# Second layer of a two-layer decoder: the softmax's inverse sums spread by DMA in place of TensorE transposes, and the outputs scaled by GpSimd

## The reference

```python
# A1: 4 groups of keys and values, 16 query heads of 64, no mask
raw  = einsum('bsgwe,btge->bstgw', Q, K * 64**-0.5)
A    = einsum('bstgw,btge->bsgwe', softmax(raw, axis=2), V).reshape(n, s, 1024)
x    = layernorm(x + (X + A @ Wpost))
# X1: 8 heads of 64, 1024 keys from the context
sim  = einsum('bihd,bjhd->bhij', q, k) * 64**-0.5
out  = einsum('bhij,bjhd->bihd', softmax(sim), v).reshape(b, n, 512)
x    = layernorm(x + out @ Wout + bout)
```

## Time and profile before

| | |
|---|---|
| runs | 1192.88, 1193.17, 1196.08 us (median 1193.17) |
| profiled execution | 1193.53 us, of which span 1191.8 us |
| mean granted TensorE clock | 0.973 |
| busy: TensorE, weight loads | 1089.6 us (91%), 689.9 us (58%) |
| busy: VectorE, ScalarE, GpSimd | 744.2 us (62%), 550.5 us (46%), 111.3 us (9%) |
| chain that ended last | PE 74%, DVE 13%, issue 5%, ACT 4%, DMA 1% |

### The profile page before, as it was taken

How to read it: one execution, slowest core, us unless ns; L and a number is a source line. 1 busy time by engine, 2 the same in 40 slices (tenths; PEclk the granted TensorE clock), 3 DMA queues, 4 the chain that set the end, 5 groups by cost and what they waited for, 6 DMA issues and landing times.

```text
span 1191.8 us, 19630 instructions
## 1 busy us (share of the span) xinstructions
PE 1089.6 (91%) x7306; PEld 689.9 (58%) x7306; DVE 744.2 (62%) x1092; ACT 550.5 (46%) x1044; POOL 111.3 (9%) x133
## 2 busy tenths in 40 slices
PE   5999989888788988789889999999999999999997
PEld 3443443432222322368666777877778787788664
DVE  3432555589999998553336566466666776776257
ACT  2434335155455556722126566356644554466320
POOL 2001123020200000010000000010002000120020
PEclk9999889799899999899999999999999999999999
DMA  5614003210000000000035333114432633220001
GB/s 153 170 71 150 10 22 112 91 65 14 14 14 14 15 1 1 1 19 1 1 72 147 72 72 72 37 45 99 107 72 54 153 88 76 68 72 1 1 1 36
DMA packets 56493, 67.89 MB, mean 57 GB/s; under 512 B 14665, under 2 KB 35922, under 8 KB 56402
## 3 DMA queue, kind: packets, MB, share of 16 engines
q1 hardware_dynamic: 55234, 65.06, 20.9%
q10 hardware_dynamic: 1168, 1.57, 0.4%
HBM read 30.96 MB, written 13.63 MB: 37 GB/s over the span
## 4 chain that ended last, share of the span: by engine, by line
PE 74%; DVE 13%; issue 5%; ACT 4%; DMA 1%; SPq 1%; ACTq 0%; POOL 0%; DVEq 0%; POOLq 0%
PE p_ring L1725 11%; PE p_unit L1725 11%; PE p_out L1872 10%; PE p_ring L1769 9%; PE p_ring L1849 9%; PE p_ring L1746 6%; PE p_out L1838 5%; PE p_ring L1815 5%; DVE halves L1496 4%; DVE prob_a L1510 2%; PE p_ring L1793 2%; DVE x L1695 2%; PE p_unit L1950 2%; ACT prob_b L1296 1%; PE p_unit L1904 1%
## 5 line engine op out<-in xcount | busy, mean ns | idle before, releaser
L1310 ACT ACTIVATE prob_a<-p_ring 128x1024 f32<-128x1024 f32 x128 | 130.5, 1022 | 97.4 <-PE p_ring L1815 97.1
L1475 DVE TENSOR_REDUCE nmax<-p_ring 128x2 f32<-128x1024 f32 (+1 forms) x128 | 156.0, 1219 | 30.1 <-PE p_ring L1769 30.1
L1496 DVE TENSOR_REDUCE halves<-p_ring 128x2 f32<-128x1024 f32 x128 | 155.8, 1220 | 27.5 <-PE p_ring L1793 27.1
L1296 ACT ACTIVATE prob_b<-p_ring,nmax 128x512 f32<-128x512 f32 (+1 forms) x192 | 158.6, 837 | 30.9 <-DVE nmax L1475 30.7
L1328 ACT ACTIVATE probT_b<-p_ring 128x512 f32<-128x512 f32 x144 | 84.5, 598 | 189.5 <-PE p_ring L1849 187.9
L1769 PE MATMUL p_ring<-stacks 128*128 128x512 f32 x512 | 150.8, 417 | 9.2 <-ACT prob_b L1296 5.4
L1529 DVE COPY probT_b<-p_ring 128x512 f32<-128x512 f32 x112 | 77.1, 688 | 114.6 <-PE p_ring L1849 114.3
L1849 PE MATMUL p_ring<-ident,prob_b 128*128 128x128 f32 x1024 | 134.6, 274 | 0.3 <-ACT probT_b L1328 0.3
L1849 PEld LDWEIGHTS p_ring<-ident,prob_b 128*128 128x128 f32 x1024 | 116.2, 141 | 23.6 <-issue 15.2
L1815 PE MATMUL p_ring<-x_q,x_kq 32*128 32x512 f32 x512 | 119.4, 648 | 2.3 <-DVE halves L1496 2.1
L1769 PEld LDWEIGHTS p_ring<-stacks 128*128 128x128 f32 x512 | 86.9, 189 | 26.2 <-ACT prob_b L1296 10.0
(11 more groups left out here) (208 smaller groups left out, 1537.9 us busy)
## 6 DMA issues: line engine op xcount, KB each, us to landing
stacks<-splitH_b SPq DMA_DIRECT2D x80, 128.0 KB, 2.3
stacks<-splitL_b SPq DMA_DIRECT2D x80, 128.0 KB, 2.4
stacks<-x_kd SPq DMA_DIRECT2D x32, 256.0 KB, 4.6
x_kd<-early SPq DMA_DIRECT2D x8, 512.0 KB, 3.8
x_v<-x_vd SPq DMA_DIRECT2D x8, 512.0 KB, 4.1
x_vd<-early SPq DMA_DIRECT2D x6, 512.0 KB, 2.8
a_st<-a_image SPq DMA_DIRECT2D x32, 64.0 KB, 2.7
x_kd<-xT SPq DMA_DIRECT2D x4, 512.0 KB, 3.1
```

What stands on the lines that cost most here:

```text
L1296: ins = nc.scalar.activation(prob_b[:, n % NP_SLOTS, a * 512:a * 512 + w_all], p_scores[:, n % 2, a * 512:a * 512 + w_all], ACT.Exp, bias= ...
L1310: nc.scalar.activation(prob_place(key), slot_of("S2", key), ACT.Exp, accum_out=x0_sums[:, m:m + 1]).then_inc(done["E2"], 1)
L1475: nc.vector.tensor_reduce(nmax[:, n % 4, 0:heads], src, AX.X, ALU.max, negate=True).then_inc(done["M"], 1)
L1496: nc.vector.tensor_reduce(to, src, AX.X, ALU.max, negate=True).then_inc(done["M1"], 1)
```

## The change

For 23 of the 24 groups the unit `rb`, `rwide` and ScalarE's copy go. VectorE's RC is the reciprocal alone. A new step RS on SyncE, in the same round, writes the inverse sums with two DMAs (one a head, 128 partitions x 4 elements of 4 bytes) to a small DRAM tensor `b_sums`, so that a head's 512 values lie in a row. Three rounds later the step RL loads each row back, repeated on 64 partitions, into one of two slots of `spread`. VectorE copies `p_out` unscaled into `outT_b` (OC) at the place where ON was, and the next group's AV waits for OC. ON is now done by GpSimd, in place on `outT_b`, and is scheduled one round after OC. The last group of all keeps `rb`; there VectorE does OC and then ON in place.

```diff
@@ stream @@
+        while spreads and spreads[0][0] <= n:
+            sched.add(*spreads.pop(0)[1])
+        while scaled and scaled[0][0] <= n:
+            sched.add(*scaled.pop(0)[1])
...
             if i == TT - 1:
-                late.append(("ON", L, b, g))
+                late.append(("OC", L, b, g))
+                scaled.append((n + 2 if (L, b, g) != last_group else n, ("ON", L, b, g)))
...
             sched.add("RC", *group)
-            sched.add("UP", "rb", *group)
-            pending.append(("rb", *group))
-            placed = True
+            if group == last_group:
+                sched.add("UP", "rb", *group)
+                pending.append(("rb", *group))
+                placed = True
+            else:
+                sched.add("RS", *group)
+                spreads.append((n + 3, ("RL", *group)))
@@ SyncE @@
+                if kind == "RS":
+                    G = group_no[key]
+                    slot, turn = G % 2, G // 2
+                    wait(sp, "RC", *key)
+                    if turn:
+                        sp.wait_ge(sums_spread[slot], 16 * 2 * turn)
+                    for a in range(2):
+                        sp.dma_start(b_sums[slot, a].rearrange("(i p) -> p i", p=128), rsum[:, slot, :, a],
+                                     allow_slow_non_contiguous=True).then_inc(sums_stored[slot], 16)
+                if kind == "RL":
+                    G = group_no[key]
+                    slot, turn = G % 2, G // 2
+                    sp.wait_ge(sums_stored[slot], 16 * 2 * (turn + 1))
+                    if turn:
+                        wait(sp, "ON", *groups[G - 2])
+                    for a in range(2):
+                        sp.dma_start(spread[64 * a:64 * a + 64, slot, :], b_sums[slot, a].partition_broadcast(64))\
+                          .then_inc(sums_spread[slot], 16)
@@ GpSimd @@
+                elif kind == "ON" and key != last_group:
+                    g = key[2]
+                    G = group_no[key]
+                    wait(pool, "OC", *key)
+                    pool.wait_ge(sums_spread[G % 2], 16 * 2 * (G // 2 + 1))
+                    nc.gpsimd.tensor_tensor(outT_b[:, g, :], outT_b[:, g, :], spread[:, G % 2, :], ALU.mult)\
+                      .then_inc(done["ON"], 1)
@@ VectorE @@
-                elif kind == "ON":
+                elif kind == "OC":
                     L, b, g = key
-                    G = group_no[key]
-                    wait(dve, "UA", "rb", *key)
                     wait(dve, "AV", *key, TT - 1, parts(key[0]) - 1)
...
-                    nc.vector.tensor_tensor(outT_b[:, g, :], p_out[:, :], spread[:, :], ALU.mult)\
+                    nc.vector.tensor_copy(outT_b[:, g, :], p_out[:, :]).then_inc(done["OC"], 1)
+                elif kind == "ON" and key == last_group:
...
+                    wait(dve, "UA", "rb", *key)
+                    wait(dve, "OC", *key)
+                    wait(dve, "ON", *groups[G - 1])
+                    nc.vector.tensor_tensor(outT_b[:, g, :], outT_b[:, g, :], spread[:, G % 2, :], ALU.mult)\
                       .then_inc(done["ON"], 1)
@@ TensorE @@
                     if i == 0 and part == 0 and G:
-                        wait(pe, "ON", *groups[G - 1])
+                        wait(pe, "OC", *groups[G - 1])
```

More of the change, by code:

```diff
@@ L266, in stream @@
     heads = [list(c) for c in chains]
-    late = []
+    late, scaled, spreads = [], [], []
+    last_group = tiles[-1][:3]
     def empty():
@@ L287, in stream @@
     n, crowded = 0, False
-    while n < len(tiles) + LAG + 1 or any(heads) or pending or late:
+    while n < len(tiles) + LAG + 1 or any(heads) or pending or late or scaled or spreads:
         if n < len(tiles):
@@ L578, in decoder @@
     bank_no = {u: i % 4 for i, u in enumerate(broad)}
-    groups = [key for kind, key in sched.steps if kind == "ON"]
+    groups = [key for kind, key in sched.steps if kind == "OC"]
+    last_group = groups[-1]
     early_places, early_uses = {}, [0] * EARLY
@@ L691, in decoder @@
         early = [early0[:, :, :], early1[:, :, :], xT[:, :, T:2 * T]]
+        b_sums = nc.dram_tensor("b_sums", (2, 2, T), F32).ap()
         x1_kd = nc.dram_tensor("x1_kd", (B, 4, 128, NKV), F32).ap()
@@ L759, in decoder @@
         x1_bo = put("x1_bo", [128, C])
-        spread = put("spread", [128, 512])
+        spread = put("spread", [128, 2, 512])
         m_b1 = put("m_b1", [128, NE + 1])
@@ L787, in decoder @@
             "E2": "turned_probs_ready", "TM": "later_keys_cleared", "PV": "values_added", "KF": "operands_rounded",
-            "RC": "sums_inverted", "ON": "outputs_scaled", "UP": "unit_ready",
[1 row of a table added]
             "UA": "unit_emptied_by_act", "UD": "unit_emptied_by_dve",
@@ L797, in decoder @@
         a0_stacked = [sem(f"a0_stacked{s}") for s in range(HELD)]
+        sums_stored = [sem(f"sums_stored{s}") for s in range(2)]
+        sums_spread = [sem(f"sums_spread{s}") for s in range(2)]
         a0_spread = [sem(f"a0_spread{b}") for b in range(B)]
@@ L1357, in _ @@
                         G = group_no[u[1:]]
-                        if G:
-                            wait(act, "ON", *groups[G - 1])
-                        ins = nc.scalar.activation(spread[:, :], p_unit[:, :], ACT.Copy)
+                        wait(act, "ON", *groups[G - 2])
+                        ins = nc.scalar.activation(spread[:, G % 2, :], p_unit[:, :], ACT.Copy)
                     elif u[0] == "xT" and u[1] == "X0":
@@ L1534, in _ @@
                     ng = LAYERS[key[0]]["G"]
[L1535 to L1542, removed]
-                elif kind == "ON":
+                    if G >= 2:
+                        dve.wait_ge(sums_stored[G % 2], 16 * 2 * (G // 2))
+                    ins = nc.vector.reciprocal(rsum[:, G % 2, :, 0:ng], sums[:, G % 2, :, 0:ng])
+                    if key == last_group:
+                        link(ins)
+                        ins = nc.vector.tensor_copy(rwide[:, :, :].rearrange("p i (a r) -> p i a r", a=ng),
+                                                    rsum[:, G % 2, :, 0:ng].unsqueeze(3).to_broadcast([128, TT, ng, 128 // ng]))
+                    ins.then_inc(done["RC"], 1)
+                elif kind == "OC":
                     L, b, g = key
-                    G = group_no[key]
-                    wait(dve, "UA", "rb", *key)
                     wait(dve, "AV", *key, TT - 1, parts(key[0]) - 1)
```

## The result

The changed kernel takes 1219.56 us (median of three runs, 1214.98 to 1224.92; a fourth, at 1233.30, counts as a slow run and is left out), the kernel before 1194.24 in the same measurement: ratio 1.0213, 95% interval 1.0184 to 1.0242. Forecast was 1184, with a range of 1178 to 1194. The profiled execution is the quickest of the runs, 1214.98 us, span 1213.2, which is 21.4 more than the span before; so the profile shows somewhat less than the median's loss of 25.

The account below looks back on a forecast made before the run. TensorE was taken to bound the kernel in the second layer's attentions. Gain 15.0 - 2.7 - 1.0 - 1.0 - 0.5 - 0.3 = 9.5 us, so 1193.5 - 9.5 = 1184.0 us, with an 8-in-10 range of 1178 to 1194.

Parts of the forecast that it names:

- Small writes: SyncE's writes of 1024 4 B elements per group: landing 4.9 us flat to 39 us linear, taken near flat.
- For traffic in the way of the stack loads: Small writes' effect on the stack loads: a charge of 1.0 us, bounds 0 and 4.
- Rival B: SyncE: stack loads queue behind the late spread load if a write takes over 22 us; 1214 us at 24; chance 0.05.
- Transposes, 15.0 us: TensorE, 23 groups losing their transposes: 15 save 0.74 us each, 8 save 0.49, together 15.0 us.
- Exchange of units, 2.7 us given back: TensorE's units sharing one PSUM bank: waits grow from 7.9 to 10.6 us in the new order.
- three second halves wait for the statistics: Output projection's second half waiting for VectorE's statistics: three places instead of one, 3 x 1.2 = 3.6 us.
- projections behind another: TensorE: three projections still stand one round behind another one, waiting 3.4 us.
- transposes of x: TensorE: 2.0 us for neighbouring transposes and the router's unit; 1.6 us for first transposes waiting for VectorE's normalisation.
- GpSimd: a multiply: GpSimd's scaling of the output, sized as half of its 128x1024 add: 1.25 us.
- Rival A: GpSimd multiplies stop VectorE's two-input operations: eight subtractions x 1.2 = 9.6 us, time 1193; chance 0.08.
- Output projections waiting for GpSimd, 1.0: TensorE at three output projections waiting for GpSimd's multiply: 0.7, 0 and 0.3 us, together 1.0.
- read-modify-write: DMA writes below 512 B: would only move the write's landing inside the three rounds before its load.

Follow-up runs that it names:

- Experiment 2: The kernel before plus each group's two scattered 4 B-element writes on SyncE, read by nobody, sums still spread by TensorE: 1223.39 us, ratio 1.0247.
- experiment 11: The changed kernel with the written elements 512 B apart and the spread load reading another tensor (outputs wrong, time only): 1181.08 us, ratio 0.9897.
- experiment 8: The kernel before plus the same touching, unread writes, issued on ScalarE's DMA queue one round later: 1234.84 us, ratio 1.0345.
- experiment 5: The changed kernel with inverse sums written as 16 B pieces and GpSimd's multiply reading them with a stride, results right: 1183.03 us, ratio 0.9915.
- Experiment 6: The changed kernel with 16 B pieces and strided multiply, and the place of rb left empty so the order of units is kept: 1181.85 us, ratio 0.9899.
- 1: The changed kernel with the small write as one DMA of 128 pieces of 32 B (sums in wrong order, time only): 1181.42 us, ratio 0.9886.
- Experiment 3: The kernel before with the raw copy on VectorE and the multiply on GpSimd, sums still spread by TensorE: 1192.61 us, ratio 0.9977.
- experiments 7 to 10: The kernel before plus unread 4 B-element writes: 512 B apart 1195.31 us; touching, on ScalarE's queue 1234.84; 64 B apart 1197.85; 16 B apart 1199.75.
- experiment 7: The kernel before plus the unread scattered writes on SyncE, each 4 B element 512 B from the next: 1195.31 us, ratio 1.0020.

## Why the prediction was wrong

**The step that failed** is "Small writes ... I take near the flat end ... For traffic in the way of the stack loads I charge 1.0 (bounds 0 and 4)". Its bracket for one write, 4.9 to 39 us, held: the two writes seen in the chain of waits took 9.64 and 11.88 us, and SyncE waited up to 11.3. Two things in it were wrong. First, the value at the flat end was an argument about latency, taken from 128 elements, for a write of 1024. A bracket that wide should have gone into the range. Second, the price on other transfers was bounded by 4 us with no row behind it. Experiment 2 puts the writes without any reader at 28 us, and experiment 11 puts them at 38 us in this kernel.

**Rival B** had the right place and the wrong condition. It let the loss begin at 22 us per write, from the slack of SyncE's queue in A1. In X1 three rounds are 8.5 us, so a write of 10 us was late there already. That its time of 1214 lies near the measured 1219.56 is luck. And it priced only the queue, while the transfers beside the writes suffered whoever issued them (experiment 8). It had a chance of 0.05, with 0.04 for its kind, on a price that no row excluded.

**The other terms held, in sum.** Without the 1.0 for small writes they give a gain of 10.5 us. The four versions with quick writes gained 10.8 (experiment 5), 11.9 (6), 13.1 (11) and 14.1 us (1). One slip: 1178, the low end of the range, is 1193.5 - 15.0 and so leaves out the exchanges too; with them in, as the text says, it is 1181. In detail:

- Transposes, 15.0 us: in X1 a pair of rounds fell from 6.39 to 5.65, as forecast. In A1 it fell by more, 6.62 to 5.70. TensorE, one such pair from one block of output matmuls to the next, before and then after:

```profile
729.85 1.97 PE L1872 MATMUL p_out<-probT_b,a_v 128*64 128x128 f32 x32
731.74 0.66 PE L1950 MATMUL p_unit<-ident,rwide 128*128 128x128 f32 x4
...
736.47 0.77 PE L1872 MATMUL p_out<-probT_b,a_v 128*64 128x128 f32 x10
```

```profile
724.19 1.97 PE L1915 MATMUL p_out<-probT_b,a_v 128*64 128x128 f32 x32
...
729.89 0.88 PE L1915 MATMUL p_out<-probT_b,a_v 128*64 128x128 f32 x12
```

- Exchange of units, 2.7 us given back: three second halves wait for the statistics for 3.7 us together (forecast 3.6), projections behind another 2.3 (forecast 3.4), transposes of x 1.4 and 0.5 (forecast 2.0 and 1.6). That is 7.9 us, no more than before, where 10.6 was forecast: nothing was given back. Experiment 6 fits: it can't tell the total from nothing.
- GpSimd: a multiply takes 1.28 us (forecast 1.25). Rival A had the mechanism right and the price wrong. Experiment 3 shows it, 2.18 us in place of 1.27 for a multiply and 2.05 in place of 1.22 for a subtraction, but in two places a subtraction and not in eight, and there was no loss. In the changed kernel the subtractions, themselves late, all took 1.21 to 1.23 us.
- Output projections waiting for GpSimd, 1.0: 6.4 in the changed kernel, and none in experiment 5. The first wait, 2.52 us, has stack issues of 3.93 us for two (at 741.87) ahead of the spread load, where 1.1 is usual; at the second, 3.92 us, the load came late behind its write. This term depended on the one that failed. The second in the chain of waits:

```profile
873.30 11.88 DMA b_sums<-rsum
```

- Not in the sum at all: the clock after a stall. TensorE's busy time fell by 3.8 us only, 1089.6 to 1085.8, where the four versions with quick writes have 1075.6 to 1078.7 with the same matmuls. So some 7 to 10 us of the loss are most likely matmuls at the lower clock.

The Trainium skill (DMA: Bandwidth & Descriptors, Specifications) says that below 512 B a transfer is done as read-modify-write. I had it move only the landing. The runs bear out that a small write can be dear, but not by its size alone: 4 B elements 512 B apart landed in 2.0 us, and 16 B pieces side by side did too. That neighbouring pieces wait for each other's read-modify-write would fit experiments 7 to 10; no run shows the inside of it.

## What to carry to other kernels

A DMA that scatters single 4 B elements so that neighbours touch in DRAM is not a 2 KB transfer: here it held up the others for up to about ten microseconds, whichever queue issued it. Let each partition write at least 16 B that lie together (the smallest piece that was tried and found quick), and let the reader undo the order with a strided view. When an operation is new to a kernel, price what it does to its neighbours as well as its own length, and if no row bounds it, let the range say so: measure it first by adding it alone to the kernel before, with nobody reading it.

## What the runs showed of the hardware

- 4 B elements side by side: 1223.39 us, 16 B apart 1199.75, 64 B apart 1197.85, 512 B apart 1195.31, against 1194 to 1196 without them; landing 3.5, 2.3 and 2.0 us for the last three.
- Such writes on one queue stretched another queue's packets from 20.9 to 25.5% of the engines' time. Behind them the DMA engines, 0.87 busy, moved 23 GB/s (187 with the elements 512 B apart), and at another place loads whose packets were all on record by 794.6 us had not landed before 802.4.
- Half as many such elements cost more (1238.17), not less.
- After waits of TensorE of 6.25 to 8.08 us the next four score matmuls took 2.04 to 2.06 us in place of 1.17 (four places in three runs); in experiment 2 the granted clock was 0.50 from 816 to 820 us, after a wait of 7.93 us. After a wait of 3.11 us (experiment 7, granted clock 1.00) they took 1.16.
- A GpSimd multiply that started 0.17 us after a VectorE subtraction with two inputs in SBUF took 2.18 us in place of 1.27; a subtraction that started 0.30 us after such a multiply took 2.05 us in place of 1.22.
- GpSimd's multiply of 128x512 read with a stride of four elements took 1.56 us, contiguous 1.28.
